# Attention's preparation of the first sequences and its first score pass, moved into the last three quarters of the first experts' rounds

## The reference, cut to what matters

```python
# layer 0
x = x + ga * mixer(layernorm(x) * (1 + ca) + sa)            # a Mamba-like mixer
h = layernorm(x) * (1 + cb) + sb
x = x + gb * (sum over 8 experts e of (w2[e] @ silu(w1[e] @ hw + b1) + b2) * (w3[e] @ hw + b3) + shared(h))
# layer 1: hw is h times the token's weight for e, both chosen experts only
h = layernorm(x) * (1 + ca) + sa
q, k, v = rope(h @ Wq), rope(h @ Wk), h @ Wv                # 16 heads of 8 channels
x = x + ga * (softmax(causal(q @ k.T / sqrt(8))) @ v) @ Wo
h = layernorm(x) * (1 + cb) + sb
x = x + gb * (the best of 8 experts of width 512 for each token)
```

## Time and profile before

| | us |
|---|---|
| median of 3 runs | 581.68 (579.49 to 581.73) |
| the profiled execution | 577.07 |
| its span, first to last instruction | 575.2 |
| PE / DVE / ACT / POOL busy | 452.4 / 392.0 / 278.1 / 271.6 |
| first experts' rounds, from the first `weigh` to the last `product` | 178.3 to 262.5 |
| preparation of attention, iterations -2 and -1 | 262.5 to 313.9 |
| iterations 0 to 16 of attention | 313.9 to about 467 |

### The profile page before, as it was taken

The page is one execution under the profiler, slowest core; times in us unless marked ns, Lnnn a source line. Parts: engine busy times, 40 slices in busy tenths (PEclk is TensorE's granted clock), DMA queues, the critical chain, the costliest instruction groups (busy, mean ns, idle before and its releaser), DMA issues.

```text
span 575.2 us, 10088 instructions
## 1 busy us (share of the span) xinstructions
PE 452.4 (79%) x3120; PEld 274.4 (48%) x3120; DVE 392.0 (68%) x1264; ACT 278.1 (48%) x518; POOL 271.6 (47%) x392
## 2 busy tenths in 40 slices
PE   3688778987998999994558998999999863059970
PEld 3545456766653444442323434435445343049970
DVE  5789738988655888886679687888898235025533
ACT  1568796653453544441223577678777831013220
POOL 4210038998301786664641047476655502714541
PEclk9988889999799999997775799999999985559995
DMA  8600000000335333310386012222300000141114
GB/s 354 169 1 1 0 2 2 1 2 1 144 148 125 99 106 99 107 62 2 108 208 124 4 31 88 82 86 85 84 5 4 3 0 10 52 123 36 36 38 146
DMA packets 25739, 39.94 MB, mean 69 GB/s; under 512 B 3228, under 2 KB 17756, under 8 KB 25164
## 3 DMA queue, kind: packets, MB, share of 16 engines
q1 hardware_dynamic: 21752, 30.42, 17.8%
q0 software_dynamic: 3936, 8.89, 5.2%
HBM read 27.55 MB, written 11.55 MB: 68 GB/s over the span
## 4 chain that ended last, share of the span: by engine, by line
PE 49%; DVE 18%; POOL 11%; issue 8%; ACT 6%; DMA 6%; SPq 0%; DVEq 0%; POOLq 0%; ACTq 0%
PE ps L1579 5%; PE ps L1581 5%; PE ps L1568 5%; PE ps L1686 4%; PE ps L1599 3%; PE ps L1771 3%; PE ps L1782 3%; POOL slots_x L586 3%; DVE rows L406 3%; PE ps L1391 2%; DVE moe L1221 2%; PE ps L1641 2%; POOL qk_parts L305 2%; DVE st L387 2%; PE ps L1672 2%
## 5 line engine op out<-in xcount | busy, mean ns | idle before, releaser
L1221 DVE CUSTOM_DVE_ANT_0 moe<-ps,const 128x512 bf16<-128x512 f32 (+3 forms) x256 | 110.5, 486 | 9.7 <-PE ps L1641 9.4
L778 ACT ACTIVATE arena<-ps 128x256 f32<-128x256 f32 (+3 forms) x128 | 85.8, 701 | 33.6 <-PE ps L1672 32.9
L476 POOL TENSOR_TENSOR arena<-arena 128x512 f32<-128x512 f32 x32 | 51.7, 1616 | 51.9 <-DVE arena L1139 51.7
L1641 PE MATMUL ps<-arena 48*128 48x128 bf16 (+3 forms) x256 | 56.1, 329 | 10.7 <-DVE arena L1221 4.7
L1672 PE MATMUL ps<-arena 51*128 51x128 bf16 (+3 forms) x256 | 52.2, 307 | 0.0
L1686 PE MATMUL ps<-arena 128*32 128x512 f32 (+3 forms) x512 | 48.4, 450 | 0.9 <-ACT arena L778 0.6
L1667 PE MATMUL ps<-bconst 64*128 64x64 bf16 x512 | 45.6, 195 | 1.2 <-ACT arena L778 0.5
L1641 PEld LDWEIGHTS ps<-arena 48*128 48x128 bf16 x256 | 16.7, 97 | 55.7 <-DVE arena L1221 31.7
L751 ACT ACTIVATE arena<-arena 128x512 f32<-128x512 f32 x32 | 20.2, 630 | 41.9 <-DVE arena L1139 41.6
L838 ACT ACTIVATE arena<-ps 128x512 f32<-128x512 f32 x23 | 13.7, 597 | 55.0 <-PE ps L1771 55.0
L592 POOL DMA_INDIRECT tokens_y<-arena,token_at x23 | 22.1, 960 | 32.5 <-DVE arena L1325 31.3
(11 more groups left out here) (239 smaller groups left out, 1113.2 us busy)
## 6 DMA issues: line engine op xcount, KB each, us to landing
arena<-expert_weights SPq DMA_DIRECT2D x32, 256.0 KB, 3.2
arena<-moe_in SPq DMA_DIRECT2D x1, 4100.0 KB, 12.8
qk_parts<-arena SPq DMA_DIRECT2D x24, 128.0 KB, 2.3
qk_parts<-arena POOLq DMA_DIRECT2D x24, 128.0 KB, 2.3
arena<-qk_parts POOLq DMA_DIRECT2D x32, 96.0 KB, 2.5
arena<-qk_parts SPq DMA_DIRECT2D x8, 288.0 KB, 5.6
moe<-moe_in SPq DMA_DIRECT2D x1, 1936.0 KB, 13.8
slots_x<-zeros SPq DMA_DIRECT2D x1, 1518.0 KB, 19.6
```

The costliest lines, as they stand in the source:

```text
L476: pool.tensor_tensor(yacc[:, ts], yacc[:, ts], pr[:, i % 2, :], ALU.add).then_inc(sem("yacc"), 1)
L778: act.activation(pt[:, u % 4, :, 0:n], ps[:, 4 + 2 * k:6 + 2 * k, 0:n], ACT.Exp, scale=ATT_SCALE).then_inc(sem("probs"), 1)
L1221: v.tensor_tensor_reduce(out=junk[:, done % 2, 0:n], in0=ps[:, k, col:col + n], in1=w["mask"][:, (3 - qt) * P:4 * P], scale=1.0, scalar=3 ...
L1641: mm = pe.matmul(ps[:, k, col:col + n], qaug[lo:lo + KR, b % 2, 2 * g + j // 2, qt * P:(qt + 1) * P], kaug[lo:lo + KR, b % 2, 2 * g + j // ...
```

## The change

All of the work of the preparation stays, but its place moves. What sequence n-1 needs is written into the rounds of sequence n (n = 1 to 3):

- e = 1: `gated`, now on ACT. e = 2: `y0_T` on PE, `residual` on DVE. e = 3: `ln_apply`. e = 4: the transpose (`x3_T`), written to `hT` by ACT.
- for n = 1 and 2, at e = 5 and 6: two `project` and two `rope` each, and a `rotate` on POOL. At e = 7 the values and the first split; the remaining splits go at e = 0, 1, 2 of the next sequence's rounds.
- in rounds 24 to 31: `scores(0, u)` and `maximum(0, u)`, slot by slot. The loop of attention begins at iteration -1.
- the last sequence's share goes into attention: `gated(3)` ahead of it, `y0_T` and `residual` at iteration 0, `ln_apply` at 2, `x3_T` at 3.
- SP does the 12 `parts_out` and 8 `relayout` of sequence 0 behind the weight row of round 22, and those of sequence 1 behind that of round 31.
- the ring has two banks (0 and 1) inside the rounds and three afterwards.
- the rotation tiles leave the first experts' weights and get room of their own. The first experts' tiles move to the arena's start, so the `moe1` weights come in four quarters, behind the small DMAs of groups 2, 4, 6 and 8.

```diff
@@ SP
+                if i in (22, DENSE - 1):
+                    b = int(i > 22)
+                    for part in range(3):
+                        parts_out(sp, b, 0, part)
+                        parts_out(sp, b, 1, part)
+                    relayout(sp, f"aug_first{b}", b, slice(0, 2))
+                    relayout(sp, ("aug0", "aug_first1")[b], b, slice(2, 8))
...
+                if s in (2, 4, 6, 8):
+                    if s == 2:
+                        sp.wait_ge(sem("x2"), B)
+                    cs = slice((s // 2 - 1) * later // 4, s // 2 * later // 4)
+                    sp.dma_start(packed["moe1"][:, cs], moe1_in[:, cs]).then_inc(sem("ld_moe1"), 16)
@@ POOL, ahead of the addition of round i = 8 n + e
+                if n >= 1 and e == 2:
+                    ln_rstd(pool, 3, n - 1)
+                if 1 <= n < 3 and e in (5, 6):
+                    rotate(2 * (n - 1) + e - 5)
+                if 1 <= n < 3 and e == 7:
+                    rest(2 * (n - 1))
+                if n >= 2 and e == 0:
+                    rest(2 * (n - 2) + 1)
+                if n >= 2 and e in (1, 2):
+                    last_part(2 * (n - 2) + e - 1)
@@ ACT, behind the silu of round i
+                if n >= 1:
+                    if e == 1:
+                        gated(n - 1)
+                    if e == 4:
+                        x3_T(n - 1)
+                if 1 <= n < 3 and e == 7:
+                    values(n - 1)
+                    part_hi(n - 1, 0)
+                if n >= 2 and e in (0, 1, 2):
+                    (part_hi, part_mid, part_mid)[e](n - 2, (1, 0, 1)[e])
@@ DVE, behind weigh(i + 1), mask(i), product(i - 1)
+                n, e = i // E0 - 1, i % E0
+                if 0 <= n < 3:
+                    if e == 2:
+                        residual(n)
+                    if e == 3:
+                        ln_apply(v, 3, x, xn, n)
+                if 0 <= n < 2 and e in (5, 6):
+                    rope(n, 2 * (e - 5))
+                    rope(n, 2 * (e - 5) + 1)
+                if 24 <= i < 32:
+                    for u in at_slot[i - 24]:
+                        maximum(0, u)
@@ PE, behind expert_out(i - 1)
+                if n >= 0:
+                    if e == 2:
+                        y0_T(n)
+                    if e == 4:
+                        x3_T(n)
+                if 0 <= n < 2:
+                    if e in (5, 6):
+                        project(n, 2 * (e - 5))
+                        project(n, 2 * (e - 5) + 1)
+                    if e == 7:
+                        project_values(n)
+                if i >= 24:
+                    for u in at_slot[i - 24]:
+                        scores(0, u)
```

More of the change, by code:

```diff
@@ L36 @@
 Z_BANK = (6, 0, 6, 0)
-Y0T_BANK = (0, 1, 6, 7)
 ROUTE0, ROUTE1 = 17, 22
@@ L464, in _, with rotate, rest, last_part @@
                     ln_rstd(pool, 2, i // TPB - 2)
+            def rotate(i):
+                a = i % 2
+                pool.wait_ge(sem("rope"), 2 * (i + 1))
+                if i >= 2:
+                    pool.wait_ge(sem("parts"), i - 1)
+                pool.tensor_tensor(qk[:, a, :], ropet[:, 2 * a, :], ropet[:, 2 * a + 1, :], ALU.add)\
+                    .then_inc(sem("qk"), 1)
+            def rest(i):
+                a = i % 2
+                pool.wait_ge(sem("part_hi"), i + 1)
+                pool.tensor_tensor(qk[:, a, :], qk[:, a, :], pc[:, a, 0, :], ALU.subtract).then_inc(sem("res"), 1)
+            def last_part(i):
+                a = i % 2
+                pool.wait_ge(sem("part_mid"), i + 1)
+                pool.tensor_tensor(pc[:, a, 2, :], qk[:, a, :], pc[:, a, 1, :], ALU.subtract).then_inc(sem("parts"), 1)
             ln_rstd(pool, 2, B - 1)
@@ L553, in late_relayout @@
                 relayout(pool, "aug_group", b, slice(2 * g, 2 * g + 2))
-            for stage in (rotate, rest, last_part):
-                stage(2)
-                stage(3)
             for it in range(-1, 15):
                 max_parts(it + 1)
+                if it == 0:
+                    ln_rstd(pool, 3, B - 1)
                 if it in (4, 5, 8, 9):
@@ L803, in _ @@
+            gated(B - 1)
+            for it in range(-1, 17):
                 for i in range(8):
+                    if (it, i) == (3, 2):
+                        x3_T(B - 1)
                     if 0 <= it < 16:
@@ L1140, in product, with rope, residual, maximum @@
                                        in1=s3[:, i % 2, :], op0=ALU.add, op1=ALU.mult).then_inc(sem("pr"), 1)
+            def rope(b, j):
+                k = ring_read(v, "rope", b, j)
+                if b >= 1:
+                    v.wait_ge(sem("qk"), 2 * (b - 1) + j // 2 + 1)
+                v.tensor_tensor(ropet[:, j, :], ps[:, k, :], w[("cos", "sin")[j % 2]], ALU.mult)\
+                    .then_inc(sem("rope"), 1)
+            def residual(n):
+                tt = slice(TPB * n, TPB * (n + 1))
+                k = ring_read(v, "y0T", n)
+                v.tensor_tensor(x[:, tt, :], x[:, tt, :], ps[:, k, :].rearrange("p (t d) -> p t d", t=TPB),
+                                ALU.add).then_inc(sem("x2"), 1)
+                v.wait_ge(sem("x2"), n + 1)
+                ln_stats(v, 3, x, n)
+                ln_moments(v, 3, n)
+            def maximum(s, u):
+                k = ring_read(v, "mx", s, u)
+                if u == 0 and s >= 2:
+                    v.wait_ge(sem("m_parts"), 4 * (s - 1))
+                col = 0
+                for c, (qt, j) in enumerate(units[u]):
+                    n = P * (qt + 1)
+                    done = 16 * s + maxima_done[u] + c
+                    if done >= 2:
+                        v.wait_ge(sem("mx"), done - 1)
+                    v.tensor_tensor_reduce(out=junk[:, done % 2, 0:n], in0=ps[:, k, col:col + n],
+                                           in1=w["mask"][:, (3 - qt) * P:4 * P], scale=1.0, scalar=3 * NEG,
+                                           op0=ALU.add, op1=ALU.max, accum_out=mx[:, s % 2, qt, j:j + 1])\
+                        .then_inc(sem("mx"), 1)
+                    col += n
             weigh(0)
@@ L1244, in attn_out @@
                     .then_inc(sem("x3"), 1)
-            for j in range(4):
-                rope(1, j)
-            ln_apply(v, 3, x, xn, 2)
-            ln_apply(v, 3, x, xn, 3)
-            for it in range(-2, 17):
+            for it in range(-1, 17):
                 for i in range(8):
+                    if (it, i) == (0, 3):
+                        residual(B - 1)
+                    if (it, i) == (2, 7):
+                        ln_apply(v, 3, x, xn, B - 1)
                     if it + 2 < 16:
```

275 lines of the change are left out of this document (103 added, 172 removed).

## The result

The kernel after takes 574.86 us (median of 8 runs, 571.02 to 578.17), the kernel before 579.14 (median of 8, 577.56 to 581.73). The ratio is 0.9922, with a 95% interval of 0.9893 to 0.995: some 4.5 us faster, where 14.2 were forecast. A second set of runs of the same pair gave 0.9926 (0.9897 to 0.9954), so the size is sure to about 2 us. Ratios are of fast runs alone, and one of the six runs of quarters_late was slow; it counts in that kernel's median only.

A forecast was written before the change was run, and what follows sets the result against it. PE was taken to pace rounds and attention, with a 52 us chain of waits between; -43.7 + 25.5 + 2.5 + 1.5 = -14.2 us from the 581.7 median gives 567.5, own range 562 to 573, 8-in-10 range 556 to 577.

The forecast's parts named there:

- C: Attention, iterations 0 to 3: added transposes on PE, a residual and four `ln_apply` on DVE cost +2.5 us (1.3 to 4.3).
- D: Attention: weight quarters fetched in iterations 1, 3, 5, 7 meet POOL's part writes in 3 and 7; +1.5 us (0 to 6.4).
- Term A: Stretch from the last product to iteration 0: shrinks from 52.2 to 8.5 us, -43.7 (bounds -44.8 and -43.2).
- Term B: First experts' rounds: they grow by +25.5 us with the moved work (bounds +16 and +31).
- Rounds 8 to 15: PE's transposes, projections and values 5.6 us, residual 0.2, `ln_apply` 1.1: +6.9 us.
- The term for the weight row: Round 23: its row, queued on SP behind 20 DMAs, comes late; 2.6 us worked out, 0 if it overtakes, 2.0 taken.
- Rounds 24 to 31: DVE paces; behind the maxima `weigh` waits for POOL's addition, such rounds take about 3.4 us: +8.9, or +4.8 without that wait.
- Most of it hides: Rival: DVE and POOL pass each other, the weight row overtakes, attention costs are low; -27.5 us, 554, around 559; chance 0.20.
- The clock: Rival: the wait for round 23's weight row drops the clock to 0.50 for the remaining rounds, +15 us, 583 to 590; chance 0.07.
- more waits: Rival: POOL steps in rounds 13 to 23 delay `weigh`, or later weight rows are late; rounds +31, about 575 us; chance 0.13.
- The change doesn't do what it says: Rival: rounds grow by as much as the stretch behind them shrinks (+40), around 581 us; chance 0.05.
- The condition that I had set for being wrong: Last product to iteration 0 over 12 us, rounds above 115 or below 100, or attention longer by more than 6 us.

The follow-up runs named there:

- quarters_late: Kernel after with the last three quarters of the `moe1` weights behind groups 11, 12 and 13 instead of 4, 6 and 8: 569.68 us, ratio 0.9853 to before.
- ln_early: Kernel after with `ln_apply` of sequence 3 moved from the last slot of iteration 2 to the first of iteration 1: 568.80 us, ratio 0.9826 to before.
- after_again: Kernel after without an edit, run and profiled a second time: ratio 0.9926 to the kernel before.
- sp_split: Kernel after with SP's 20 DMAs of sequence 0 spread behind the weight rows of rounds 22, 23 and 27: 564.94 us, ratio 0.977 to before.
- weigh_first: Kernel after with the maxima of rounds 24 to 31 one round later, between `weigh` and `mask`: 576.02 us, ratio 0.9949 to before.
- both_attn: Kernel after with the edits of ln_early and quarters_late together: 564.97 us, ratio 0.974 to before.

## Why the prediction was wrong

The direction and the mechanism were right: a stretch of 52 us in which every engine waited for another became 8.2 us, at the price of longer rounds. The size was wrong, -14.2 forecast and -4.3 to -4.7 measured. The time forecast, 567.5, missed the 574.86 by 7.4 us only, because the median that I started from (581.7, of 3 runs) was 2.5 above the 579.14 of 8 runs. That is luck.

**The step that failed** is the one of terms C and D, +2.5 "of which DVE's idle quarter hides a part" and +1.5 for the quarters: +4.0, measured +11.4. Neither meeting is large in itself. In C I priced `ln_apply` at its length of 1.09, with the row of 6.50 for eight beside it in the same group, and did not ask what POOL does at (iteration 2, slot 7). It was splitting sequence 2 then. In D I did name the mechanism, the quarters that move while POOL writes out parts, and sized the longer wait of POOL. But I named two of its places and wrote that there is no such wait for the first two quarters. Before, POOL's first relayout of sequence 2 waited 1.31 us too, at 358.10, and behind the second quarter it waits 2.6 to 4.3 in the profiles, against 1.3 to 2.8 without it; the third quarter meets the relayouts in iteration 5. What both sums left out is what comes behind: PE waits about 2 us, and the clock is at half for 3.4 to 17 us after it. ln_early and quarters_late take away one meeting each, and 6.6 and 5.6 us of attention go with them. Without both, attention is +1.8 to +2.3, close to the +2.5 that C gave for the moved work. That the fall of the clock follows from the meeting and its wait is shown as far as it can be here: in all six kernels in which one or both of the meetings were taken away the fall at that place went too, and where a meeting was left it stayed. The length of the wait alone does not decide it: 1.39 us at iteration 9 of after_again had a fall behind it, and 1.41 us in the rounds of sp_split, at 241.8, had none. How long a fall lasts at one place differs from run to run, and I have no cause for that.

The Trainium skill ("SBUF — State Buffer", section "Who interferes with whom") counts VectorE's tensor_scalar, which `ln_apply` is, among the instructions that can take the port pair shared with GpSimd, and has the first taker keep it for its whole instruction. I had used this section for the rounds and not for attention. The row at 334.51 goes further than that: 2.37 us is longer than any one instruction of POOL there, two DMA issues of 0.53 and a `rotate` of 1.27. It ends 0.11 us behind the `rotate`, which started 0.99 behind it. Which of the three held it no run separates.

For the parts, the same skill ("DMA: Bandwidth & Descriptors", section "Issuing engines are not separate DMA queues") says that DMAs of different issuers run on the same 16 engines and interleave. The trace agrees, with POOL's 4.05 us of wait beside a transfer that SP issued, against 1.33 without it.

**Term A, the gap.** Forecast 8.5, measured 8.2 in both profiles and between 8.2 and 8.4 in all kernels. Right.

**Term B, the rounds.** Forecast +25.5, measured +27.5 (111.0 less 83.5). By sequence, cut at the starts of products 8, 16 and 24 (cut one product earlier, 0.7 us more of the difference falls to the last column and 0.7 less to the third):

| us | rounds 0 to 7 | 8 to 15 | 16 to 23 | 24 to 31 |
|---|---|---|---|---|
| forecast | 0 | +6.9 | +9.7 | +8.9 |
| measured | 0 | +6.7 | +13.8 | +7.0 |

*Rounds 8 to 15.* Right, and `ln_apply` took 2.13 of the forecast 2.4 in this one (2.91 in the next sequence, 2.06 in the last).

*Rounds 16 to 23.* The term for the weight row was mis-sized: 2.0 forecast, 5.5 measured. The working up to it held. SP was free 15.0 us after the start of round 18, where 7.8 and 6.9 make 14.7. The row then landed 22.5 us after that start, where I had 21.3. So PE lost 3.5 in place of the 2.6 of the working, which I had cut to 2.0 in case the row overtook, and the clock fell for 3.4 us at 260.9, which I had left out. sp_split takes all of it away. The rest of these rounds is then +8.2 with the forecast at +7.7.

*Rounds 24 to 31.* +7.0 in place of +8.9, and by another engine than I said. I had DVE pacing at 3.4 us, through `weigh` behind POOL's addition. The wait is there (1.37 us for 0.68). But weigh_first takes it away without a gain, and it costs 0.13 us of a round, so it was not what set the pace. PE set it, with 3.1 us, since scores between fp32 matmuls cost more than their own length: ten units at 0.5 and two sets of transposes at 0.63 make +6.3 of the +7.0. Here two errors had opposite signs.

**The rivals.** *Most of it hides* fell: neither the weight row nor the meetings hid. *The clock* came true in kind, in the rounds for 3.4 us only (6.8 in ln_early and both_attn), and the price I gave it (+15) was for a fall that lasts; its real harm was in attention, where I had not looked. Of the *more waits*, the time of 575 is what was measured, but its place is another: the rounds stood at +27.5 and not at +31, and attention at +11.4 and not at +6.5 (2.5 and 4). That the sums meet is luck. *The change doesn't do what it says* fell: the stretch shrank by 44 and the rounds grew by 27.

The condition that I had set for being wrong, attention longer by more than 6 us, was met. The other two were not (gap under 12, rounds between 100 and 115).

**Open.** The tail is 1.3 us longer after, with a stretch of 3.4 us at half clock in it that before doesn't have; whether the change brings it isn't settled, and no kernel was made for it. Six of the ten profiles of changed kernels have the stretch, and PE's waits ahead of it in after, 0.60 to 0.72 us, are those of before. Nor is it settled why iteration 0 takes 12.6 us after and 10.5 or 11.6 before; it starts with the clock low in both kernels.

## What to carry to other kernels

When work is moved into a stage that another engine paces, look at each moved instruction's slot for what the neighbour engine and the DMA queues do just then, not only for whether there is idle time in the stage: a shift of fifteen slots for four instructions of 0.34 us was worth 5.6 us here, and one of a transfer's place 2 to 4. Price each new wait of PE of about 2 us in such a stage at up to three times its length, as at iteration 3 here (2.47 us of wait, 4.5 to 7.8 lost), since the clock can fall behind it. In an in-order DMA queue, spread a block of 20 DMAs between the small loads that somebody waits for: it cost a few moved lines and gave 5.5 us of the rounds.

## What the runs showed that I had not expected

- A VectorE tensor_scalar of 128x128 that takes 0.34 us alone was held for 2.37 us while GpSimd issued two DMAs and ran one tensor operation, so across three instructions of GpSimd.
- bf16 scores between fp32 matmuls of 512 columns: the matmul ahead of them starts its successor 0.95 us later and the one behind them 0.96, where fp32 behind fp32 takes 0.86. With the 0.32 of the scores, a unit costs about 0.5 us.
- A weight row of 256 KB that is issued behind eight relayouts on the same queue landed after 7.4 us, where the median is 3.3.
- Waits of PE of 1.3 to 3.5 us, in stretches where it is otherwise nearly always busy, were followed by 3.4 to 17 us at 1.2 GHz; one of 1.41 us was not. In after and after_again, one program, the stretch at iteration 3 lasted 6.8 and 17.1 us. The rounds begin anywhere between 178.3 and 183.4 us, and the time at half clock ahead of them doesn't order that: 27.3 us of it go with 178.3 and with 181.3.
